# Routing table made between two products' low halves, group words loaded one group ahead, 47 narrow products of zeros, final wait moved from GpSimd to VectorE

## What is computed

```python
x = x + xattn(layernorm(x), ctx, ctx, Wq, bq, Wk, bk, Wv, bv, We, be)   # 16 heads of 16
x = x + ffn(layernorm(x), router_w, router_b, expert_up, expert_down)

def ffn(x):                                    # 8 experts, 256 -> 1024 -> 256
    probs = softmax(x_flat @ router_w + router_b)
    top_w, top_idx = top_k(probs, 2)
    comb = sum(top_w[..., None] * one_hot(top_idx, 8), axis=1)
    for e in range(8):
        h = gelu(x_flat @ expert_up[e].T)      # exact gelu
        out_e = h @ expert_down[e].T
        output += comb[:, e:e + 1] * out_e
```

## Time and profile before

| what | value |
|---|---|
| timed runs | 412.85, 411.17, 406.46 us; median 411.17 us |
| the profiled execution: its own time | 409.87 us |
| its span, first to last instruction | 407.9 us |
| mean granted TensorE clock over the span | 0.978 |
| busy, share of the span: PE / PEld / DVE / ACT / POOL | 89% / 78% / 60% / 44% / 39% |

### The profile page before, as it was taken

How to read it: one execution, slowest core, us unless ns; L and a number is a source line. 1 busy time by engine, 2 the same in 40 slices (tenths; PEclk the granted TensorE clock), 3 DMA queues, 4 the chain that set the end, 5 groups by cost and what they waited for, 6 DMA issues and landing times.

```text
span 407.9 us, 8337 instructions
## 1 busy us (share of the span) xinstructions
PE 362.7 (89%) x2474; PEld 317.7 (78%) x2475; DVE 242.9 (60%) x692; ACT 180.2 (44%) x283; POOL 159.8 (39%) x190
## 2 busy tenths in 40 slices
PE   6999988988988889896799999999999999999970
PEld 4765675665676559895699999999999999999970
DVE  4694776899799858764323657365565365243330
ACT  2654435344434345431523855638384284253320
POOL 2324021202302041142454556474838628616640
PEclk9999999999999999989899999999999999999996
DMA  8912010401221121451321384564829404404221
GB/s 269 353 66 103 0 54 0 157 13 41 69 89 52 53 55 53 145 168 25 45 46 47 55 242 153 131 201 83 247 30 266 65 0 67 63 0 63 46 38 22
DMA packets 26484, 37.49 MB, mean 92 GB/s; under 512 B 4737, under 2 KB 17473, under 8 KB 26465
## 3 DMA queue, kind: packets, MB, share of 16 engines
q1 hardware_dynamic: 19312, 26.98, 19.8%
q0 software_dynamic: 7152, 10.27, 14.3%
HBM read 27.45 MB, written 9.79 MB: 91 GB/s over the span
## 4 chain that ended last, share of the span: by engine, by line
PE 64%; DVE 17%; issue 7%; POOL 4%; ACT 3%; DMA 1%; POOLq 1%; DVEq 0%; ACTq 0%
PE bankC L1250 11%; PE bankC L1251 9%; PE bankC L1252 9%; PE bankD L1612 5%; PE bankD L1614 5%; PE bankD L1613 5%; DVE nmax L799 3%; PE bankA L1344 2%; POOL rstd L374 2%; PE bankC L1612 2%; PE bankA L1580 1%; DVE put L964 1%; DVE stat L758 1%; PE bankC L1345 1%; PE bankC L1613 1%
## 5 line engine op out<-in xcount | busy, mean ns | idle before, releaser
L1250 PE MATMUL bankC<-xnT_h,up_w 128*128 128x256 f32 (+1 forms) x240 | 75.8, 316 | 6.9 <-issue 6.8
L701 ACT ACTIVATE hh<-bankC 128x512 fp32r<-128x512 f32 (+1 forms) x52 | 36.2, 697 | 99.6 <-PE bankC L1252 99.6
L1251 PE MATMUL bankC<-xnT_l,up_w 128*128 128x256 f32 (+1 forms) x240 | 73.7, 307 | 0.0
L1252 PE MATMUL bankC<-xnT_h,up_w 128*128 128x256 f32 (+1 forms) x240 | 73.5, 306 | 0.0
L1612 PE MATMUL bankD<-dn_w,hh 128*128 x208 | 59.5, 286 | 0.3 <-DVE hl L1181 0.2
L1613 PE MATMUL bankD<-dn_w,hh 128*128 x208 | 58.8, 282 | 0.0
L1614 PE MATMUL bankD<-dn_w,hl 128*128 x208 | 58.7, 282 | 0.0
L450 POOL DMA_INDIRECT xr<-rows,idx_g x37 | 49.2, 1330 | 15.8 <-issue 15.0
L1250 PEld LDWEIGHTS bankC<-xnT_h,up_w 128*128 128x128 f32 x240 | 46.3, 193 | 9.4 <-issue 9.1
L1181 DVE TENSOR_TENSOR hl<-prob,hh 128x512 fp32r<-128x512 f32 (+1 forms) x26 | 21.3, 820 | 53.0 <-ACT prob L702 53.0
L1252 PEld LDWEIGHTS bankC<-xnT_h,up_w 128*128 128x128 f32 x240 | 46.4, 193 | 0.0
(11 more groups left out here) (310 smaller groups left out, 841.8 us busy)
## 6 DMA issues: line engine op xcount, KB each, us to landing
xall<-up SPq DMA_DIRECT2D x24, 256.0 KB, 3.8
xall<-down SPq DMA_DIRECT2D x24, 256.0 KB
rows<-xr SPq DMA_DIRECT2D x4, 528.0 KB, 3.2
raw<-up SPq DMA_DIRECT2D x4, 512.0 KB, 4.8
raw<-down SPq DMA_DIRECT2D x4, 512.0 KB, 5.5
out<-xall SPq DMA_DIRECT2D x4, 512.0 KB, 2.8
xall<-x SPq DMA_DIRECT2D x1, 1536.0 KB, 8.2
cst<-const SPq DMA_DIRECT2D x1, 640.0 KB, 8.1
```

What stands on the lines that cost most here:

```text
L701: a.activation(hT_h[:, 2 * q:2 * q + 2, 0:n * P], bank, ACT.Gelu)
L1250: mm(out_, left_h, right_h, start=first, stop=False)
L1251: mm(out_, left_h, right_l, start=False, stop=False)
L1252: return mm(out_, left_l, right_h, start=False, stop=last)
```

## The change

Five edits. (1) On VectorE the first two low halves of expert 1 stay where they were, the third goes behind the first twelve operations of the table, the fourth behind the next eight; `table_turn` on TensorE moves two hidden tiles (six products) forward, and the copy to `tab` goes ahead of `x_low_f(0, 0)`. (2) PE's word of a unit is loaded one unit ahead, into a register, between the down products of tile 0 and tile 1. (3) 47 products of zeros with 32 columns moving are put ahead of the 15 with 512. (4) The last unit no longer gathers for the unit two behind it. (5) The final load and wait for `d_add` move from GpSimd to VectorE.

```diff
--- before.py
+++ after.py
@@ -475,7 +475,8 @@
                 word = pool_word(u)
                 base = word // 4 % 64
                 g.tensor_copy(idx_s[:, 3 * ring:3 * ring + 3], slot[:, bass.ds(word // 256, 3)]).then_inc(g_si, 1)
-                gather(u + 2, ring)
+                with pool.If(nu > u + 1):
+                    gather(u + 2, ring)
                 pool.wait_ge(g_si, u + 1)
 
                 pool.wait_ge(d_add, 16 * base + 64)
@@ -507,8 +508,6 @@
                     add(u, 0)
                     with pool.If(nu > u + 1):
                         add(u + 1, 1)
-            total = pool.value_load(tbase_i[:, bass.ds(nu + 1, 1)], min_val=0, max_val=NT)
-            pool.wait_ge(d_add, 16 * total + 64)
 
 
         @block.scalar
@@ -1086,8 +1085,8 @@
                 .then_inc(v_slot, 1)
             v.tensor_scalar(slot[:, NE * COLS:MAPC], c("iota")[:, 0:32], 0.0, c("spare"), ALU.mult, ALU.add)\
                 .then_inc(v_slot, 1)
-            for b in range(4):
-                h_low_early(1, b)
+            h_low_early(1, 0)
+            h_low_early(1, 1)
             dve.wait_ge(v_done, 1)
             v.tensor_reduce(ntile[:, :], big[:, :, :], AX_X, ALU.add).then_inc(v_table, 1)
             v.tensor_reduce(units[:, :], big[:, :, 0:COLS - 1:2], AX_X, ALU.add).then_inc(v_table, 1)
@@ -1107,6 +1106,7 @@
             v.tensor_copy(pack[:, 5:8], uend[:, NE - 1:NE].broadcast_to([P, 3])).then_inc(v_table, 1)
             v.scalar_tensor_tensor(out=mix[:, :], in0=odd[:, :], scalar=2.0, in1=alone[:, :],
                                    op0=ALU.mult, op1=ALU.add).then_inc(v_table, 1)
+            h_low_early(1, 2)
             dve.wait_ge(v_table, 12)
 
 
@@ -1117,6 +1117,7 @@
                                          (onm, "tile", ALU.is_equal, mix[:, :])):
                 v.scalar_tensor_tensor(out=part[:, :], in0=ubeg[:, :], scalar=c(at), in1=factor,
                                        op0=op, op1=ALU.mult).then_inc(v_table, 1)
+            h_low_early(1, 3)
             dve.wait_ge(v_table, 20)
             for one, part, op in ((te1, on, ALU.add), (tb, onb, ALU.max), (tt, ont, ALU.max), (tpar, onf, ALU.add),
                                   (tprev, onp, ALU.add), (tthree, onq, ALU.add), (todd, ono, ALU.add),
@@ -1170,9 +1171,9 @@
                 dve.wait_ge(a_fxT, u + 1)
                 v.tensor_tensor(xT_l, bankA[:, :, 0:TRI], xT_h.bitcast(F32), ALU.subtract).then_inc(v_fxT, 1)
 
-            x_low_f(0, 0)
             dve.wait_ge(p_tab, 1)
             v.tensor_copy(tab[:, :], bankM[0:8, 0:NTAB]).then_inc(v_tab, 1)
+            x_low_f(0, 0)
 
 
             def h_low(u, n):
@@ -1239,6 +1240,10 @@
                     unit(u, 0)
                     with dve.If(nu > u + 1):
                         unit(u + 1, 1)
+
+            total = dve.value_load(tbase_i[:, bass.ds(nu + 1, 1)], min_val=0, max_val=NT)
+            dve.wait_ge(d_add, 16 * total + 64)
+            settle(16)
 
         @block.tensor
         def _(pe):
@@ -1445,6 +1450,8 @@
                     mm(bankC[:, bank, :], zero_r[:, :], zeros, start=True, stop=True)
 
             pe.wait_ge(g_zero, 2)
+            for _ in range(47):
+                mm(bankC[:, 2, 0:32], zero_r[:, :], zero_r[:, 0:32], start=True, stop=True)
             keep_busy(2, 15)
             pe.wait_ge(d_const, 16)
             x_turn(0, 0)
@@ -1535,7 +1542,7 @@
                 for m in range(KF):
                     if t == 0 and m % 2 == 0:
                         pe.wait_ge(v_he, 4 * e + m // 2 + 1)
-                    if e and t and m == KF - 2:
+                    if e and t and m == KF // 2:
                         table_turn()
                     h = slice((2 * m + t) * P, (2 * m + t + 1) * P)
                     mm(out_, he_h[:, h], dn_w[:, e, m, 0, :], start=(m == 0), stop=False)
@@ -1618,9 +1625,15 @@
             pe.wait_ge(v_tab, 1)
             nu = pe.value_load(nu_i, min_val=NE, max_val=NU)
 
+            def table_word(u):
+                return pe.value_load(w_i[:, bass.ds(u, 1)], min_val=0, max_val=64 * NT + 63)
+
+
+            next_word = pe.alloc_register("next_word")
+            pe.reg_mov(next_word, table_word(0))
             with pe.Fori(0, NU) as u:
                 with pe.If(nu > u):
-                    word = pe.value_load(w_i[:, bass.ds(u, 1)], min_val=0, max_val=64 * NT + 63)
+                    word = pe.snap(next_word, min_val=0, max_val=64 * NT + 63)
                     e, three_, par = word // 4 % 8, word // 2 % 2, word % 2
                     pe.wait_ge(v_wlo, 4 * e + 2)
                     pe.wait_ge(v_fxT, u + 1)
@@ -1640,6 +1653,7 @@
                         pe.wait_ge(a_gelu, 4 * u + 5)
                         down_tile(u, par, 2, True)
                     down_tile(u, par, 0, True).then_inc(p_dn0, 1)
+                    pe.reg_mov(next_word, table_word(u + 1))
                     down_tile(u, par, 1, False).then_inc(p_dn, 1)
```

## The result

| | before | after |
|---|---|---|
| median of the timed runs beside each other (18 each) | 411.2 us | 406.06 us |
| ratio of the two | | 0.9928, 95% interval 0.9902 to 0.9954 |
| the profiled execution: its own time | 409.87 us | 406.0 us |
| its span | 407.9 us | 403.5 us |
| mean granted clock | 0.978 | 0.988 |

The account below looks back on a forecast made before the run. TensorE was taken to bound the kernel, with 64% of the chain of waits. Terms -2.1 - 2.2 - 1.4 - 0.8 - 3.0 + 2.0 - 2.2 = -9.7 gave 400.2 us profiled, 401.5 as median; range 397.5 to 407.5.

Parts of the forecast that it names:

- 47 narrow products: At TensorE's start: the added products delay the first transposes, and so every engine, by 2.0 us.
- Rival D: At the start: narrow products don't lift the clock, the start comes 4 to 7.5 us late, 404 to 407; chance 0.13.
- The code block: Unit 0's 2.785 us branch is a wait for code; 94 instructions ahead move it away, -2.2 us.
- Rival B: The code wait only moves to another branch or into the down products, the clock falls as before: 405; chance 0.20.
- Its price and the clock's: Unit 0: -2.2 us for the branch, -1.4 for the half clock behind it, -0.8 for the one after the first hole.
- term of 1.4 us for the half clock behind the branch: Unit 0's down products: with the hole gone, the half clock of 202.17 to 205.58 goes too, -1.4 us.
- Clock at unit 0: Half clock of 191.93 to 195.34 follows the hole ahead of unit 0, which shrinks; half of its 1.7 counted, -0.8 us.
- Table: Before unit 0: table made between the low halves, `tab` ready 2.2 us sooner, unit 0's first product 2.1 us sooner.
- End: GpSimd's drain keeps its length and begins behind its last add, at 398.8 instead of 401.0: -2.2 us.
- rival C: At the end: the drain waits for the landing of the adds, GpSimd's end stays where it was, 403.7; chance 0.12.
- Rival E: The loop, now spanning four code blocks, no longer stays in instruction memory; 12 passes pay 2.6 us each, 433; chance 0.05.
- Word a unit ahead: Boundaries between units: the word's load leaves the loop's head, six boundaries at 0.5 us, -3.0 us; bounds 0 and 5.5.

Follow-up runs that it names:

- the jump of 94 and of 256: Changed kernel with 47 or 128 narrow products (94 or 256 instructions) behind the wide ones and always jumped over: ratios 0.9769 and 0.9827 to the kernel before.
- the last run: Changed kernel without narrow products, none jumped over either, and with the transfers of zeros behind the first raw weights: 401.5 us, ratio 0.9767 to the kernel before.

## Why the prediction was wrong

**47 narrow products: the step that failed.** "By the loads, 14 fit until 4.2, 33 more at 0.107 take 3.5, and 15 wide at 0.23 another 3.5." The duration of one, 0.213 at half clock from the load rows, was right (10.05 / 47 = 0.214). The time at which the clock rises was taken from the wide products of before, 4.2 us, as if it followed from TensorE being busy. Under narrow products it did not rise at all: all 47 ran at half pace, and then the 15 wide ones had to bring it up, nine of them at half pace. +7.7 instead of +2.0, and 2.0 had already been chosen below the 2.5 of its own sum. Rival D had this mechanism and the right size, "4 to 7.5 us late", with a chance of 0.13. Its time, 404 to 407, holds the result, and the range held it by that rival. That the time lies in the range is rival D's doing and not the forecast's. What was needed was in the rows: the trace of before shows the clock rising under products with 512 columns (at 4.2 us) and with 256 (at 195.34, in the up products), and nowhere under narrower ones alone, so a rise at 4.2 us under 32 columns was a supposition and not a reading. The bounds of the term, 0 to 2.5, should have been 0 to 7.5.

**The code block: right.** The branch was a wait for code, the 94 instructions moved it away, and the jump of 94 and of 256 showed it from both sides. Rival B fell: no other branch took its place, and no hole in unit 0's down products is above 0.52 us. **Its price and the clock's: right in sum by luck.** Unit 0, from its first up product to that of unit 1, was to shrink by 2.2 + 1.4 + 0.8 = 4.4 us and shrank by 4.15, but its parts are others:

| part of unit 0 | before | after | difference | predicted |
|---|---|---|---|---|
| up products (first half clock) | 7.17 | 5.63 | -1.5 | -0.8 |
| last up product to first down product (branch) | 3.79 | 1.16 | -2.6 | -2.2 |
| down products (second half clock) | 7.10 | 7.13 | 0 | -1.4 |

The term of 1.4 us for the half clock behind the branch failed as a term: the down products were no faster without it. The run without narrow products says the same, 7.01 us from its first down product to unit 1, at half clock for 2.8 of them. Branch and second half clock together are worth 3.0 us by the unit of 16.92 or 16.91 us with both against 13.92, and 3.8 by 18.07 against the 14.31 of the kernel before with narrow products.

**Clock at unit 0:** -0.8 predicted; -1.15 (18.07 - 16.92) where the long branch follows, -0.4 (14.31 against 13.92) where it does not. So the half clock's price depends on what comes behind it. Nor is it bound to the hole: with a hole of 2.9 us a half clock followed in the kernel before and in two of its variants, with one of 2.77 us it did not.

**Table:** -2.1 predicted, -2.1 across the change and -2.24 alone, by the traces (the timed runs of the table alone can't tell it from nothing). **End:** -2.2, it was -2.7; rival C fell, as the drain begins while the last add is still on its way (VectorE's wait for it ends at 399.13, two microseconds into the drain). **Rival E** fell: the loop spans a block more, three packets come in unit 0 and none after that, and no branch in 13 units is above 0.36 us. By the two-page window of the Trainium skill, "Runtime: NRT & Kernel Launch", section "Instruction fetch mechanics", each pass would stall; the trace disagrees here as it did before.

**Word a unit ahead:** -3.0 predicted, -3.1 and -3.2 measured, but not by the path described. The prediction had "Six boundaries at 0.5" and, in two-tile units, tile 1 starting 0.7 us late, so that "little is won". All twelve boundaries became shorter, by 0.06 to 0.77 us, 5.0 us in all, of which 2.2 behind two-tile units; tile 1 starts 0.05 to 0.45 us late in every unit, and that took 1.9 us back. That the sum agrees so well is luck. The bounds, 0 and 5.5, were right.

So the steps on table, code, word and end held in size, and the narrow products took back more than half of what the others gained. The single edits agree: word -5.0, end -2.7, table -1.1 and narrow products +4.2 us by their ratios sum to -4.5 us, with intervals of about 2 us to either side on each; 3 us were measured, and the spans of the two profiled executions differ by 4.4.

**Open.** What makes the clock fall in attention in one execution and not in another, as at 96.08, 131.86, 133.62 and 142.11 us, is not settled, and no run takes it away. It does go with the spread of a kernel's executions, 2 to 7 us: of the 39 executions of the kernel before in the experiments, the four with a mean granted clock of 0.986 took 406.6 to 407.5 us, the nine at 0.970 or less 411.0 to 413.3. Why SyncE's hold on the last transfer of zeros is 3.84 us in one trace and 4.98 in another is open too.

## What to carry to other kernels

A clock that rises under one kind of work has been read for that kind only: where a change puts another kind in its place, the bound of its price is that the clock never rises. Instructions placed ahead of a loop act in two ways, by running and by lying there, and a jump over them tells these apart and can give the second for nothing. Where a sum comes out right, its parts are still to be measured one by one. A step that starts earlier brings no more than the next late transfer allows, so the waits of the stretch behind it are to be listed before its gain is counted.

## What was not expected of the hardware

- With 15 wide products from a cold start, the clock rose 2.9 to 6.2 us after the first, from one kernel's trace to another.
- Products of zeros with 32 or with 128 columns, back to back for 10 us, left TensorE at half pace, and with 32 columns the clock fell from full to half under them. 62 with 256 columns raised it at 6.67 us.
- At half clock products with a load of 128 x 128 each are 0.212 to 0.214 us apart whether 32, 128 or 256 columns move, and the loads fill that time (48 loads busy for 10.04 us): with few columns it is not the columns that set the pace.
- 94 instructions ahead of the loop removed a branch of 2.8 to 3.3 us, and 256 brought one of 3.2 back.
- GpSimd's drain takes 6.2 to 6.4 us, with an add in flight or not; only its start can be moved.
- What a half clock of 3.41 us cost differs from place to place: 1.6 us at 27.33 of the run with the jump, 0.4 in unit 0 without a long branch, 0.3 at 133.62 of the last run, and nothing that can be seen in unit 0's down products.
